# First attention layer of an audio tower: softmax sums inverted by VectorE block transposes, exponentials pre-added on GpSimd, weight scale from ScalarE sums

## The chip, the core and the metric

One NeuronCore of a Trainium2 chip runs the whole program. Its five engines have queues of their own: TensorE (PE, with its weight loads as PEld), VectorE (DVE), ScalarE (ACT), GpSimd (POOL) and SyncE (SP), which here only issues DMAs. Each engine executes its queue strictly in the order in which the program wrote it, and semaphores tie the queues together. The metric is the device time of one execution in microseconds; the median of three runs is 1176.59 us (1174.29 to 1178.07).

## The reference, cut to what matters

The input x has the shape (64, 96, 512): for each of 64 samples 32 channels of q, of k and of v over 512 positions. The first layer is an attention without heads over these, and it is the only part that the change touches:

```python
weight = jnp.einsum('bct,bcs->bts', q * scale, k * scale)   # 64 x 512 x 512
weight = jax.nn.softmax(weight, axis=-1)
h = jnp.einsum('bts,bcs->bct', weight, v)                   # 64 x 32 x 512
```

Then h, seen as 2048 rows of 512, goes through a layer norm, grouped-query attention with rotary embedding within each sample's 32 rows, a residual, a second layer norm and a gated feed-forward layer whose weights are quantized to -1, 0 and 1 by a threshold that is half the mean of |w|:

```python
h = h + attn(layernorm(h), Wq, Wk, Wv, Wo)
h = h + bitlinear(sigmoid(bitlinear(x, w1)) * bitlinear(x, w2), w3)
```

The preparation of both sets of weights runs inside the first part of the kernel.

## The kernel before, in words

The program has two stages. `token_attention` computes the first layer for 16 groups of four samples and prepares the weights beside it; `blocks` then runs the two other layers over 16 tiles of 128 rows. Between them all engines meet at a barrier. Only `token_attention` is changed.

**One group in `token_attention`.** A group has 16 score tiles of 128 x 512 in each of two forms. The *row* form (`rows`, line 469) has a query position on each partition and serves only to find the maximum of each row on VectorE (`maximum`, line 334). The *column* form (`cols`, line 492) has key positions on the partitions; two more rows of its operands carry the negated maxima, so ScalarE can take exponentials straight from PSUM (`exps`, line 293). q and k are split into a high and a low part so that 96 contraction rows of one fp32r product carry the precision: ScalarE rounds (`split_high`, line 287), GpSimd subtracts (`split_low`, line 248), and six SBUF to SBUF DMAs interleave the parts (`stack`, lines 175 to 180). The tiles `raw`, `high` and `low` are separate, so the next `load_qk` (line 166) waits only for `lo_done`.

**Values and sums.** For each of four blocks of key positions `values` (line 512) multiplies the exponentials by v, into OUT, and once more by a matrix of ones, into DEN: eight calls per group, at the steps of `VALUES_AT`. Each call is four fp32 matmuls of 32 output partitions. Then DEN has to be inverted and brought into the layout of OUT: ScalarE copies DEN and OUT to SBUF (lines 324 and 327), TensorE picks one row per sample and transposes it (`pick`, line 488, 16 matmuls with 4 columns), VectorE takes the reciprocal of 128 x 16 (`invert`, line 357), TensorE spreads it again (`spread_inverses`, line 521, 16 matmuls with 128 columns), and VectorE multiplies (`finish`, line 363).

**The order of work** is written out by hand. TensorE runs a loop of 16 steps per group (`step`, line 526). Step u of loop g issues one row tile and one column tile: at u = 2 to 11 rows 6 to 15 of group g+1, at u = 12 to 17 rows 0 to 5 of group g+2, and columns u of group g (u = 16 and 17 are columns 0 and 1 of group g+1). Row tiles go through a ring of three PSUM banks (`enter_ring`, line 463), so row tile n waits until VectorE has reduced row tile n-3. Column tiles have three banks too. The picks and spreads of group g-1 come at u = 4 and 5 of loop g. VectorE's loop (line 444) finishes rows 14 and 15 of group g+1, splits the maxima (lines 340 and 343), then reduces rows 0 to 13 of group g+2, with `take_transposed` (line 352) behind row 1, `invert` behind row 8 and `finish` behind row 9.

**Weights.** The attention weights (20 pieces of 128 x 1024) stay in SBUF; in loops 0 to 4 VectorE finds their largest magnitude (`largest`, line 367), and from loop 6 GpSimd scales them (`scale_attn`, line 253), ScalarE rounds them to fp16 (`attn_high`, line 305) and GpSimd computes the rest (`attn_low`, line 257). The feed-forward weights (12 pieces of 128 x 1408) are loaded twice: in loops 0 to 5 ScalarE sums their magnitudes (`measure_ffn`, line 298), and from loop 6 VectorE makes them ternary with two passes per piece (`below`, line 372, `above`, line 377). Before loop 6 VectorE runs `scales` (line 380), a chain of small operations with two GpSimd reductions over the partitions inside it.

## Time and profile before

| | |
|---|---|
| median of 3 runs | 1176.59 us (1174.29 to 1178.07) |
| profiled execution, its own time | 1181.81 us |
| its span, first to last instruction | 1179.9 us |
| PE busy in the span | 1097.3 us (93%) |
| DVE, POOL, ACT busy | 722.2, 433.5, 422.4 us |
| `token_attention` | 0 to 395.7 us, when the first load of `blocks` is issued |
| mean granted TensorE clock | 0.964 of full speed |

A busy share is an average over both stages. Matmuls are pipelined and their ends are modelled, so a busy PE need not be one that works at its peak. In a row of the trace the number in front is the start, the next one the duration; what stands in brackets is the idle time before it and what ended it. The granted clock is given as a share of full speed, 2.4 GHz; 0.5 is the lower level, 1.2 GHz.

### The profile page before, as it was taken

The numbers are of one execution on the slowest core, as the hardware profiler recorded it, in microseconds if no ns is written. First come the engines' busy times: TensorE is split into PE (matmuls) and PEld (weight loads), VectorE is DVE, ScalarE is ACT, GpSimd is POOL, SyncE is SP. The second block draws the span as 40 slices with busy tenths as digits, with TensorE's granted clock in tenths as the row PEclk, the third lists the DMA queues.
The fourth block names the chain that finished last, engine by engine and source line by source line (L and its number), as shares of the span: only waits on it lengthen the run. The fifth ranks groups of instructions, "written<-read, shape, count | busy, mean of one in ns | idle before, by whom it ended". The sixth has DMA issues, their size and how long they took to land.

```text
span 1179.9 us, 22172 instructions
## 1 busy us (share of the span) xinstructions
PE 1097.3 (93%) x8768; PEld 609.3 (52%) x8768; DVE 722.2 (61%) x1293; ACT 422.4 (36%) x733; POOL 433.5 (37%) x334
## 2 busy tenths in 40 slices
PE   4999998889989569999999999999999999999987
PEld 2434333343334234664665756646646657566465
DVE  6687766766686255556655755665566557656642
ACT  1666545545555221322322412323223223223231
POOL 2001016664555254242351451433423614524320
PEclk9999898989998779999999999999999999999999
DMA  6988833554442100000000000000000000000000
GB/s 181 315 298 260 299 115 115 158 176 124 140 130 69 57 9 10 20 9 27 18 9 27 0 27 18 9 27 18 9 27 18 9 27 0 27 18 9 18 11 9
DMA packets 35767, 83.81 MB, mean 71 GB/s; under 512 B 4496, under 2 KB 5264, under 8 KB 35728
## 3 DMA queue, kind: packets, MB, share of 16 engines
q1 hardware_dynamic: 35728, 83.26, 22.8%
q8 instruction: 27, 0.44, 0.2%
q14 instruction: 12, 0.10, 0.0%
HBM read 49.43 MB, written 8.39 MB: 49 GB/s over the span
## 4 chain that ended last, share of the span: by engine, by line
PE 51%; DVE 8%; issue 4%; POOL 2%; ACT 0%; DMA 0%; SPq 0%; DVEq 0%; POOLq 0%
PE proj L973 7%; PE proj L974 7%; PE proj L975 7%; PE ffn_sum L1025 5%; PE ffn_sum L1026 5%; PE proj L1087 4%; PE proj L1088 4%; PE proj L1089 4%; PE transposed L967 3%; PE ffn_sum L1073 2%; PE transposed L1041 1%; PE proj L1059 1%; PE proj L1060 1%; DVE probs_t L930 1%; DVE scores L910 1%
## 5 line engine op out<-in xcount | busy, mean ns | idle before, releaser
L334 DVE TENSOR_REDUCE row_max<-score_rows 128x1 f32<-128x512 f32 x256 | 167.7, 686 | 94.0 <-PE score_rows L474 92.6
L700 POOL TENSOR_TENSOR roped<-rope_cos,rope_sin 128x512 f32<-128x512 f32 x80 | 101.7, 1271 | 328.3 <-DVE rope_sin L836 328.3
L293 ACT ACTIVATE exps<-score_cols 128x512 f32<-128x512 f32 x256 | 146.2, 600 | 140.4 <-PE score_cols L499 137.9
L1025 PE MATMUL ffn_sum<-x_hi,ffn_w 128*128 128x128 f16 x1408 | 167.0, 220 | 1.4 <-ACT x_hi L769 1.4
L1026 PE MATMUL ffn_sum<-x_lo,ffn_w 128*128 128x128 f16 x1408 | 166.8, 220 | 0.0
L735 ACT ACTIVATE squares<-proj 128x512 f32<-128x512 f32 x80 | 47.8, 597 | 323.4 <-PE proj L975 289.5
L973 PE MATMUL proj<-attn_slots,x_hi 128*128 128x512 f16 x384 | 147.8, 385 | 3.7 <-DVE rope_sin L836 2.2
L974 PE MATMUL proj<-attn_slots,x_hi 128*128 128x512 f16 x384 | 147.7, 385 | 0.0
L975 PE MATMUL proj<-attn_slots,x_lo 128*128 128x512 f16 x384 | 147.5, 384 | 0.0
L474 PE MATMUL score_rows<-k_parts,q_parts 96*128 96x512 f32 x256 | 127.4, 511 | 16.5 <-DMA k_parts<-qk_low 15.2
L1025 PEld LDWEIGHTS ffn_sum<-x_hi,ffn_w 128*128 128x128 f16 x1408 | 138.1, 98 | 6.4 <-DVE hidden L853 3.0
L1026 PEld LDWEIGHTS ffn_sum<-x_lo,ffn_w 128*128 128x128 f16 x1408 | 138.5, 98 | 2.3
L474 PEld LDWEIGHTS score_rows<-k_parts,q_parts 96*128 96x128 f32 x256 | 53.7, 211 | 133.8 <-DVE row_max L334 72.6
L499 PE MATMUL score_cols<-q_parts,k_parts 98*128 98x512 f32 x256 | 110.2, 436 | 8.8 <-DMA q_parts<-max_t 6.9
L1087 PE MATMUL proj<-attn_slots,ctx_hi 128*128 128x512 f16 x256 | 97.0, 379 | 2.6 <-DVE ctx_lo L867 2.6
L1089 PE MATMUL proj<-attn_slots,ctx_lo 128*128 128x512 f16 x256 | 97.0, 379 | 0.0
L1088 PE MATMUL proj<-attn_slots,ctx_hi 128*128 128x512 f16 x256 | 97.0, 379 | 0.0
L248 POOL TENSOR_TENSOR qk_low<-qk_raw,qk_high 128x1024 fp32r<-128x1024 f32 x16 | 38.9, 2431 | 149.2 <-ACT qk_high L287 149.2
L707 POOL TENSOR_TENSOR roped<-roped,rms_inv 128x512 f32<-128x512 f32 x80 | 83.3, 1041 | 11.5
L703 POOL TENSOR_TENSOR rms_inv<-mean_sq,minus_half 128x4 f32<-128x4 f32 x80 | 85.2, 1065 | 3.3
L832 DVE TENSOR_TENSOR rope_cos<-proj,tables 128x512 f32<-128x512 f32 x80 | 55.1, 689 | 47.2 <-ACT squares L735 47.1
L853 DVE SCALAR_TENSOR_TENSOR hidden<-tanh,ffn_sum 128x512 f32<-128x512 f32 (+1 forms) x48 | 30.8, 641 | 85.7 <-PE ffn_sum L1026 85.7
(108 smaller groups left out, 1724.7 us busy)
## 6 DMA issues: line engine op xcount, KB each, us to landing
raw_ffn<-in_w_ffn SPq DMA_DIRECT2D x24, 704.0 KB, 7.2
attn_slots<-in_w_attn SPq DMA_DIRECT2D x20, 512.0 KB, 10.8
qk_raw<-in_qk SPq DMA_DIRECT2D x16, 512.0 KB, 5.8
q_parts<-qk_high SPq DMA_DIRECT2D x32, 256.0 KB, 3.3
k_parts<-qk_high SPq DMA_DIRECT2D x32, 256.0 KB, 4.2
v_t<-in_v_t SPq DMA_DIRECT2D x16, 256.0 KB, 5.7
q_parts<-qk_low SPq DMA_DIRECT2D x16, 256.0 KB, 4.9
k_parts<-qk_low SPq DMA_DIRECT2D x16, 256.0 KB, 5.2
```

What stands on the lines that cost most here:

```text
L293: nc.scalar.activation(E[:, (STEPS * g + u) % NE, :], ST[(STEPS * g + u) % 3][:, :], ACT.Exp, scale=TOK_SCALE).then_inc(exp_done, 1)
L334: nc.vector.reduce_max(row_max[:, g % 2, k:k + 1], S[n % NS][:, :], AX.X).then_inc(s_free, 1)
L474: nc.tensor.matmul(bank[:, :], QP[g % NB][0:3 * CH, b, t * P:(t + 1) * P], KP[g % NB][0:3 * CH, b, :], start=True, stop=True).then_inc(s_f ...
L499: nc.tensor.matmul(ST[n % 3][:, :], KP[g % NB][0:3 * CH + 2, b, i * P:(i + 1) * P], QP[g % NB][0:3 * CH + 2, b, :], start=True, stop=True) ...
L973: nc.tensor.matmul(dst, ah, bh, start=(i == 0), stop=False)
L974: nc.tensor.matmul(dst, ah, bl, start=False, stop=False)
L975: t = nc.tensor.matmul(dst, al, bh, start=False, stop=(i == len(pairs) - 1))
L1025: nc.tensor.matmul(dst, w, x2h[:, k * P:(k + 1) * P], start=(k == 0), stop=False)
L1026: ins = nc.tensor.matmul(dst, w, x2l[:, k * P:(k + 1) * P], start=False, stop=(k == KD - 1))
L1087: nc.tensor.matmul(PROJ[1][:, :], ah, bh, start=(k == 0), stop=False)
L1088: nc.tensor.matmul(PROJ[1][:, :], ah, bl, start=False, stop=False)
L1089: ins = nc.tensor.matmul(PROJ[1][:, :], al, bh, start=False, stop=(k == HEADS - 1))
```

## The change

It does seven things, all in `token_attention`.

1. **Inverse of the sums.** `pick`, `spread_inverses` and both ScalarE copies go. VectorE transposes DEN in 32 x 32 blocks into `den_t`, takes the reciprocal of one column of each block, transposes a broadcast of it back (`turn_sums`, `invert`), and multiplies OUT, now read in PSUM, by it (`finish`). These stand behind rows 8, 9 and 10.
2. **Pre-added exponentials.** GpSimd adds the exponentials of key blocks 0 and 1 (`sum_pair`), and in groups with `DEPTH` 2 (0 to 7, 14 and 15) those of block 2 (`sum_third`). TensorE multiplies the sum by the ones once (`total(g, None)`); the blocks left over go one by one. `values` becomes `weigh` (OUT, steps 8, 10, 13, 17) and `total` (DEN, steps 15 and 18 at depth 2, steps 12, 15 and 18 at depth 1; step 18 is step 2 of the next loop).
3. **Bound of the attention weights.** VectorE's `largest` goes; ScalarE sums the magnitudes (`bound_attn`), two or three pieces a loop in loops 0 to 7.
4. **Scaling of the attention weights.** GpSimd's `scale_attn` goes; ScalarE writes the scaled piece twice, once as fp16 and once as fp32, in loops 9 to 15.
5. **Ternary pass.** One piece per loop in loops 8 to 13, and three each in loops 14 and 15; the three of loop 15 stand behind the last `finish`. `scales` moves from loop 6 to loop 8.
6. **One in-place tile for the split.** `raw`, `high` and `low` become one tile `qk_split`; low overwrites raw. `load_qk(g)` now waits until the six copies of group g-1 have landed.
7. **SP's order.** Weight loads for loop g+1 are issued in loop g and ahead of `load_qk(g + 3)`; the last ternary loads stand ahead of the last `store_h`.

```diff
...
-        PICK_AT, SPREAD_AT = 4, 5
-        VALUES_AT = [7, 9, 10, 11, 13, 15, 16, 17]
-        SPLIT_AT = 14
         EARLY = 14
-        MEASURE_AT, CONVERT_AT = [12, 16], [11, 16]
-        MEASURED = 6
+        MEASURED = 8
         SCALED = 14
-        A_MEASURED = [range(4 * g, 4 * g + 4) if g < A_CHUNKS // 4 else () for g in range(NG)]
-        F_MEASURED = [range(2 * g, 2 * g + 2) if g < MEASURED else () for g in range(NG)]
-        A_CONVERTED = [range(2 * (g - MEASURED), 2 * (g - MEASURED) + 2) if g >= MEASURED else () for g in range(NG)]
-        F_CONVERTED = [()] * MEASURED + [(0,), (1,), (2,), (3,), (4,), (5,), (6, 7), (8, 9), (10,), (11,)]
+        SPLIT_AT = 13
+        A_MEASURE_AT, F_MEASURE_AT, CONVERT_AT = (3, 8, 12), (5, 15), (3, 12, 16)
+        A_MEASURED = shares([2, 3] * 4 + [0] * 8)
+        F_MEASURED = shares([2, 1] * 4 + [0] * 8)
+        A_CONVERTED = shares([0] * 9 + [2, 3, 3, 3, 3, 3, 3])
+        F_CONVERTED = shares([0] * 8 + [1] * 6 + [3, 3])
+        BEFORE_TAIL = 6
+        DEPTH = [2] * 8 + [1] * 6 + [2] * 2
+        SUMS_BEFORE = [sum(GB * d for d in DEPTH[:g]) for g in range(NG + 1)]
+        DENS_BEFORE = [sum(NT - d for d in DEPTH[:g]) for g in range(NG + 1)]
+        OUT_AT = {8: 0, 10: 1, 13: 2, 17: 3}
+        DEN_AT = {1: {12: None, 15: 2, 18: 3}, 2: {15: None, 18: 3}}
...
             def load_qk(g):
-                if g > 0:
-                    sp.wait_ge(lo_done, g)
-                sp.dma_start(raw[:, :, :], qk[g, :, :, :]).then_inc(qk_in, DMA)
+                if g == 2:
+                    sp.wait_ge(stacked[0], copies(0))
+                elif g > 2:
+                    sp.wait_ge(stacked[(g - 1) % 2], copies(g - 1))
+                sp.dma_start(split_raw(g), qk_raw[g, :, :, :]).then_inc(qk_in[g % 2], DMA)
...
             for g in range(NG):
                 if g + 2 < NG:
                     stack(g + 2)
+                if 0 < g and g + 1 < NG:
+                    load_v(g + 1)
+                for c in A_MEASURED[g + 1] if g + 1 < NG else ():
+                    load_attn(c)
+                for c in F_MEASURED[g + 1] if g + 1 < NG else ():
+                    measure_ffn(c)
+                early = F_CONVERTED[g] if g < NG - 2 else F_CONVERTED[g][:2] if g == NG - 2 else ()
+                for c in early:
+                    convert_ffn(c)
                 if g + 3 < NG:
                     load_qk(g + 3)
-                if 0 < g and g + 1 < NG:
-                    load_v(g + 1)
-                for c in F_MEASURED[g]:
-                    measure_ffn(c)
-                for c in F_CONVERTED[g]:
-                    convert_ffn(c)
-                for c in A_MEASURED[g]:
-                    load_attn(c)
                 if g > 0:
                     store_h(g - 1)
                 if g + 1 < NG:
                     store_max(g + 1)
+                for c in F_CONVERTED[g][len(early):]:
+                    convert_ffn(c)
             store_h(NG - 1)
             sp.wait_ge(h_out, NG * DMA)
...
+            def sum_pair(g, b):
+                pool.wait_ge(exp_done, STEPS * g + GB + b + 1)
+                if g > 0 and b == 0:
+                    pool.wait_ge(den_done, DENS_BEFORE[g - 1] + 1)
+                first = (STEPS * g + b) % NE
+                second = (STEPS * g + GB + b) % NE
+                nc.gpsimd.tensor_tensor(SUM[:, b, :], E[:, first, :], E[:, second, :], ALU.add).then_inc(summed, 1)
+
+            def sum_third(g, b):
+                pool.wait_ge(exp_done, STEPS * g + 2 * GB + b + 1)
+                pool.wait_ge(summed, SUMS_BEFORE[g] + b + 1)
+                third = (STEPS * g + 2 * GB + b) % NE
+                nc.gpsimd.tensor_tensor(SUM[:, b, :], SUM[:, b, :], E[:, third, :], ALU.add).then_inc(summed, 1)
...
+                for c in A_CONVERTED[g][:1]:
+                    attn_low(c)
+                for b in range(GB):
+                    sum_pair(g, b)
+                if DEPTH[g] == 2:
+                    for b in range(GB):
+                        sum_third(g, b)
                 if g == MEASURED:
                     reduce_partitions()
-                for c in A_CONVERTED[g]:
-                    scale_attn(c)
-                for c in A_CONVERTED[g][:1]:
+                for c in A_CONVERTED[g][1:2]:
                     attn_low(c)
                 if g + 3 < NG:
-                    split_low(g + 3)
-                for c in A_CONVERTED[g][1:]:
+                    lower(g + 3)
+                for c in A_CONVERTED[g][2:]:
                     attn_low(c)
...
+            def bound_attn(c):
+                act.wait_ge(a_in[c % NA], DMA * (c // NA + 1))
+                nc.scalar.activation(W.attn[:, 0:A_CHUNK], W.raw(c), ACT.Abs, accum_out=bound[:, c:c + 1]
+                                     ).then_inc(a_stat, 1)
...
             def attn_high(c):
-                act.wait_ge(a_scaled, c + 1)
+                act.wait_ge(chain, SCALED)
                 if c > 0:
                     act.wait_ge(a_lo, c)
-                nc.scalar.copy(W.hi(c * A_CHUNK, A_CHUNK), W.raw(c)).then_inc(a_hi, 1)
+                scale = scale_of[:, c:c + 1]
+                nc.scalar.activation(W.hi(c * A_CHUNK, A_CHUNK), W.raw(c), ACT.Copy, scale=scale).then_inc(a_hi, 1)
+                nc.scalar.activation(W.raw(c), W.raw(c), ACT.Copy, scale=scale).then_inc(a_scaled, 1)
...
+            def turn_sums(g):
+                dve.wait_ge(den_done, DENS_BEFORE[g + 1])
+                nc.vector.transpose(den_t[:, :, :].rearrange("p k c -> p (k c)"), DEN[:, :]).then_inc(den_turned, 1)
+
             def invert(g):
-                n = ring["pick", g]
-                dve.wait_ge(s_full, n + 1)
-                nc.vector.reciprocal(rden[:, :, :].rearrange("p i b -> p (i b)"), S[n % NS][:, 0:STEPS]
-                                     ).then_inc(s_free, 1)
+                dve.wait_ge(den_turned, g + 1)
+                nc.vector.reciprocal(rden[:, :], den_t[:, :, 0]).then_inc(inverted, 1)
+                dve.wait_ge(inverted, g + 1)
+                nc.vector.transpose(den_t[:, :, :].rearrange("p k c -> p (k c)"),
+                                    rden[:, :].unsqueeze(2).to_broadcast([P, STEPS, CH])).then_inc(inverse_out, 1)
 
             def finish(g):
-                dve.wait_ge(spread, g + 1)
-                dve.wait_ge(sums_out, 2 * g + 2)
-                nc.vector.tensor_tensor(out[:, :], out[:, :], DEN[:, :], ALU.mult).then_inc(h_done, 1)
...
+                dve.wait_ge(inverse_out, g + 1)
+                dve.wait_ge(out_done, NT * (g + 1))
+                if g > 0:
+                    dve.wait_ge(h_out, DMA * g)
+                nc.vector.tensor_tensor(out[:, :], OUT[:, :], den_t[:, :, :].rearrange("p k c -> p (k c)"), ALU.mult
+                                        ).then_inc(h_done, 1)
...
+                    for c in F_CONVERTED[g] if k == 3 and g < NG - 2 else ():
+                        below(c)
+                    for c in F_CONVERTED[g] if k == 5 and g < NG - 2 else ():
+                        above(c)
+                    for c in F_CONVERTED[g][:2] if k == 5 and g == NG - 2 else ():
+                        below(c)
+                        above(c)
+                    if k == 8:
+                        turn_sums(g)
+                    if k == 9:
                         invert(g)
-                    if k == PICK_ROW:
+                    if k == 10:
                         finish(g)
+                for c in F_CONVERTED[g][2:] if g == NG - 2 else F_CONVERTED[g] if g == NG - 1 else ():
+                    below(c)
+                    above(c)
...
+            def weigh(g, i):
+                if i == 0:
                     if g > 0:
-                        pe.wait_ge(sums_out, 2 * g)
+                        pe.wait_ge(h_done, g)
                     pe.wait_ge(v_in[g % NV], DMA * (g // NV + 1))
                 pe.wait_ge(exp_done, STEPS * g + GB * (i + 1))
                 for b in range(GB):
-                    into, by = (DEN, ones[:, :]) if sums else (OUT, VT[g % NV][:, i, b * CH:(b + 1) * CH])
-                    last = nc.tensor.matmul(into[b * CH:(b + 1) * CH, :], by, E[:, (STEPS * g + GB * i + b) % NE, :],
-                                            start=(i == 0), stop=(i == NT - 1))
...
+                last.then_inc(out_done, 1)
+
+            def total(g, i):
+                if i is None:
+                    if g > 0:
+                        pe.wait_ge(den_turned, g)
+                    pe.wait_ge(summed, SUMS_BEFORE[g + 1])
+                else:
+                    pe.wait_ge(exp_done, STEPS * g + GB * (i + 1))
+                for b in range(GB):
+                    of = SUM[:, b, :] if i is None else E[:, (STEPS * g + GB * i + b) % NE, :]
+                    last = nc.tensor.matmul(DEN[b * CH:(b + 1) * CH, :], ones[:, :], of, start=(i is None),
+                                            stop=(i == NT - 1))
+                last.then_inc(den_done, 1)
...
+                if u in OUT_AT:
+                    weigh(g, OUT_AT[u])
+                if u in DEN_AT[DEPTH[g]]:
+                    total(g, DEN_AT[DEPTH[g]][u])
+                if g > 0 and u + STEPS in DEN_AT[DEPTH[g - 1]]:
+                    total(g - 1, DEN_AT[DEPTH[g - 1]][u + STEPS])
...
```

## Rows read from the trace of the kernel before

**Rows 1.** The page's slices: granted clock, tenths of full speed, 40 slices.

```profile
PEclk9999898989998779999999999999999999999999
```

**Rows 2.** Busy time from finish to finish: PE, PEld, DVE, ACT, POOL; clock, DMA.

```profile
56.27:75.98 19.71, 19.71 (x140) 8.37 (x139) 16.12 (x27) 13.43 (x23) 2.39 (x1) 1.00 0.83 273
...
216.42:239.78 23.36, 21.28 (x139) 9.20 (x139) 16.27 (x23) 12.91 (x21) 13.55 (x6) 0.94 0.49 141
...
359.55:377.88 18.33, 18.33 (x129) 7.33 (x130) 12.05 (x16) 11.67 (x20) 6.18 (x3) 0.95 0.17 56
```

**Rows 3.** TensorE in time order, loop 1: start, duration, instruction.

```profile
50.36 0.40 PE L499 MATMUL score_cols<-q_parts,k_parts 98*128 98x512 f32 x1
...
51.69 0.50 PE L474 MATMUL score_rows<-k_parts,q_parts 96*128 96x512 f32 x1
52.03 0.40 PE L499 MATMUL score_cols<-q_parts,k_parts 98*128 98x512 f32 x1
52.26 0.40 PE L474 MATMUL score_rows<-k_parts,q_parts 96*128 96x512 f32 x1
...
55.68 0.50 PE L474 MATMUL score_rows<-k_parts,q_parts 96*128 96x512 f32 x1
```

**Rows 4.** Groups by line: count | busy us, mean ns | idle us.

```profile
L700 POOL TENSOR_TENSOR roped<-rope_cos,rope_sin 128x512 f32<-128x512 f32 x80 | 101.7, 1271 | 328.3 <-DVE rope_sin L836 328.3
...
L248 POOL TENSOR_TENSOR qk_low<-qk_raw,qk_high 128x1024 fp32r<-128x1024 f32 x16 | 38.9, 2431 | 149.2 <-ACT qk_high L287 149.2
...
L305 ACT CAST attn_slots<-attn_slots 128x1024 f16<-128x1024 f32 x20 | 20.8, 1038 | 8.0 <-POOL attn_slots L253 8.0
...
L372 DVE TENSOR_SCALAR ffn_w<-raw_ffn,w_nthr_of 128x1408 f16<-128x1408 f32 x12 | 14.3, 1190 | 0.0
...
L910 DVE STREAM_TRANSPOSE scores<-transposed 128x512 f32<-128x512 f32 x16 | 11.5, 717 | 12.6 <-PE transposed L1041 12.6
...
L357 DVE RECIPROCAL tok_rden<-score_rows 128x16 f32<-128x16 f32 x16 | 4.1, 258 | 13.7 <-PE score_rows L488 13.4
```

**Rows 5.** All engines in time order around one `above`.

```profile
208.59 2.14 POOL L257 TENSOR_TENSOR attn_slots<-attn_slots 128x1024 f16<-128x1024 f32 x1
...
208.69 3.53 DVE L377 SCALAR_TENSOR_TENSOR ffn_w<-raw_ffn,w_thr_of,ffn_w 128x1408 f16<-128x1408 f32 x1
...
212.14 1.87 DVE L334 TENSOR_REDUCE row_max<-score_rows 128x1 f32<-128x512 f32 x3
...
212.97 1.03 PE L488 MATMUL score_rows<-tok_ident,tok_den_sum 128*128 128x4 f32 x8 [2.08 <-DVE row_max L334]
```

**Rows 6.** Busy time and granted clock after that wait, same columns as group 2.

```profile
212.50:216.00 3.50, 3.03 (x42) 2.61 (x42) 2.47 (x5) 0.60 (x1) 3.50 (x2) 0.80 1.06 321
216.00:219.50 3.50, 3.50 (x21) 1.62 (x14) 2.08 (x3) 1.19 (x2) 1.75 (x1) 0.71 0.67 259
```

**Rows 7.** One line of VectorE, `above`: duration min/median/max.

```profile
L377 DVE SCALAR_TENSOR_TENSOR ffn_w<-raw_ffn,w_thr_of,ffn_w x12: 1675/3315/3527, 185.2 to 379.6; 128x1408 f16<-128x1408 f32 x12
```

**Rows 8.** VectorE in time order around `scales`.

```profile
166.42 0.34 DVE L384 TENSOR_REDUCE w_amax<-w_amax 128x1 f32<-128x8 f32 x4
...
171.41 1.29 DVE L334 TENSOR_REDUCE row_max<-score_rows 128x1 f32<-128x512 f32 x2
```

**Rows 9.** The page's DMA issues: count, KB each, median us to landing.

```profile
raw_ffn<-in_w_ffn SPq DMA_DIRECT2D x24, 704.0 KB, 7.2
attn_slots<-in_w_attn SPq DMA_DIRECT2D x20, 512.0 KB, 10.8
qk_raw<-in_qk SPq DMA_DIRECT2D x16, 512.0 KB, 5.8
...
k_parts<-qk_low SPq DMA_DIRECT2D x16, 256.0 KB, 5.2
```

**Rows 10.** All engines in time order at the end of the stage.

```profile
392.51 0.69 DVE L363 TENSOR_TENSOR tok_out_sum<-tok_out_sum,tok_den 128x512 f32<-128x512 f32 x1 [1.29 <-PE tok_den L521]
...
395.67 0.34 SPq L673 DMA_DIRECT2D h_ln<-h_rows  x1
```

More of the change, by code:

```diff
@@ L67, in ternary, with shares, token_attention @@
         return self.ffn[:, c * F_CHUNK:(c + 1) * F_CHUNK]
-LOOK, MAXIMA_AT, PICK_ROW = 6, 2, 9
+LOOK, MAXIMA_AT = 6, 2
 def score_ring():
     order = {}
-    for period in range(NG + 2):
+    for period in range(NG + 1):
         rows = [("row", period, k) for k in range(STEPS)] if period < NG else []
         maxima = [("max", period - 1)] if 1 <= period <= NG else []
-        pick = [("pick", period - 2)] if period >= 2 else []
-        for entry in rows[:MAXIMA_AT] + maxima + rows[MAXIMA_AT:PICK_ROW] + pick + rows[PICK_ROW:]:
+        for entry in rows[:MAXIMA_AT] + maxima + rows[MAXIMA_AT:]:
             order[entry] = len(order)
     return order
-def token_attention(nc, qk, vt, h1, ident_in, W, w_attn, w_ffn):
+def shares(counts):
+    ends = [sum(counts[:n + 1]) for n in range(len(counts))]
+    return [range(end - count, end) for count, end in zip(counts, ends)]
+def token_attention(nc, qk_raw, vt, h1, ident_in, W, w_attn, w_ffn):
     with ExitStack() as ctx:
@@ L100, in token_attention @@
         VT = [sb(f"v_t{n}", [P, NT, P]) for n in range(NV)]
[L101 to L102 removed]
+        qk = sb("qk_split", [P, 4, T])
         E = sb("exps", [P, NE, T])
+        SUM = sb("exp_sums", [P, GB, T])
         ident = sb("tok_ident", [P, P])
@@ L423, in scales @@
                 link(last)
-            def weights(g, k):
-                if k in (1, 5, 9, 13) and A_MEASURED[g]:
-                    largest(A_MEASURED[g][k // 4])
-                for n, c in enumerate(F_CONVERTED[g]):
-                    if k == (3, 10)[n]:
-                        below(c)
-                    if k == (5, 12)[n]:
-                        above(c)
             nc.vector.memset(ones[:, :], 1.0).then_inc(const_set, 1)
@@ L481, in transpose_maxima @@
                                  start=True, stop=True).then_inc(s_full, 1)
-            def pick(g):
-                pe.wait_ge(sums_out, 2 * g + 1)
-                bank = enter_ring(ring["pick", g])
-                first = ident[:, :].rearrange("p (b c) -> p b c", c=CH)[:, :, 0]
-                for i in range(NT):
-                    last = nc.tensor.matmul(bank[:, i * GB:(i + 1) * GB], den[:, i * P:(i + 1) * P], first,
-                                            start=True, stop=True)
-                last.then_inc(s_full, 1)
             def cols(g, u):
@@ L549, in _ @@
             cols(0, 1)
-            for g in range(NG + 1):
+            for g in range(NG):
                 for u in range(2, STEPS + 2):
-                    if g < NG:
-                        step(g, u)
-                    if u == PICK_AT and g > 0:
-                        pick(g - 1)
-                    if u == SPREAD_AT and g > 0:
-                        spread_inverses(g - 1)
+                    step(g, u)
+            total(NG - 1, NT - 1)
 TOK = 64 * 32
```

198 lines of the change are left out of this document (106 added, 92 removed).

## The prediction, made before the changed kernel was run

> **What bounds the kernel now.** I read the slices first, to see where the granted clock leaves its full level: only in the first third, which is `token_attention` [rows 1]. The second stage is not touched by the change, so all that counts is the first 395.7 us. Cut from one `finish` to the next, that stage gives 15 loops. A loop with nothing in its way takes 19.7 us, PE is busy in all of it, and VectorE, ScalarE and GpSimd are not (16.1, 13.4 and 2.4 us) [rows 2]. So TensorE's content is the bound there. The loops with ternary passes take about 23.4; of the six whole ones five lie between 23.2 and 23.4 [rows 2].
>
> Why 23.4 and not 19.7: VectorE's `above` stands 3.5 us instead of 1.7, because a GpSimd subtraction had begun 0.1 us before it; the row ring runs dry and PE idles 2.08 us [rows 5, 7]. Then the clock falls to its lower level: the two stretches behind it show 0.80 and 0.71, so 0.20 x 3.5 + 0.29 x 3.5 = 1.7 us of full-speed work is lost [rows 6]. 19.7 + 2.1 + 1.7 = 23.5. This is the pattern for what follows: a wait of 2 us of PE costs nearly 4.
>
> **What the change takes off TensorE.** From a column tile ahead of a `values` call to the row tile behind it are 1.33 us instead of 0.23, and the next pair costs 0.34 instead of 0.23: 1.2 us per call. From the row tile at 52.26 to that at 55.68 are 3.42 us; six row and column tiles of 0.235 are 1.41, so `pick` and `spread_inverses` are 2.0 [rows 3]. At depth 2 eight calls become six: 2.4 + 2.0 = 4.4 off, 15.3 us of PE content. At depth 1 seven are left: 16.5 us.
>
> **What takes its place.** The first `weigh` of a loop (u = 8) waits for `h_done` of the group before. VectorE reaches it through this chain: row tile 7 is issued behind the last `total`, 1.7 us into the loop, its maximum starts at 2.2; maxima 7 to 10 take 4 x 0.6 (three in 1.87, [rows 5]); two block transposes at 0.72 and a reciprocal at 0.26 [rows 4]; the multiply 0.69 [rows 10]; about 0.2 for semaphores, less about 0.3 that neighbours overlap. 2.2 + 2.4 + 1.4 + 0.3 + 0.7 = 7.0 us. PE gets there after 1.7 + 5.5 pairs of 0.47 = 4.3 to 4.5. So it idles 2.5 us, in order, with every row and column tile queued behind the waiting matmul, and ScalarE behind those. Before, `pick` and `finish` had no such chain and the loop had no wait. And 2.5 us is longer than the 2.08 after which the clock fell, so I add 1.7.
>
> **GpSimd's share.** It ran one instruction in a measuring loop; now there are eight additions of 1.27 us and the subtraction of 2.4 [rows 4], 12.6 us, two thirds of the loop. They hide beside PE: pairs end near 9 us, thirds near 13.5, `total` asks for them at u = 15, about 15 us in. What isn't hidden is the wait of VectorE for them. The row for `above` shows median 3.3 against a minimum of 1.7 [rows 7]. The second max split and `above` read two SBUF tiles; the split stands right ahead of the transposition of the maxima on PE. No row shows a split beside a GpSimd instruction: the ends are nothing (no loop is longer, as none was) and two instructions of 1.27, 2.5 us per loop. I take 0.6, half an addition, since GpSimd is idle a third of the time and PE has a little slack. By the Trainium skill (SBUF — State Buffer, Who interferes with whom) a VectorE instruction with two SBUF inputs and a GpSimd instruction that reads SBUF exclude each other for the whole of the one that came first, while a reduction never takes part; the 3.5 us row agrees, and by that rule the block transposes and `finish` stay free, but each split can lose up to a whole addition.
>
> Measuring loop: 15.3 + 2.5 + 1.7 + 0.6 = 20.1 us. Converting loop: 16.5 + 2.5 + 1.7 + 0.6, and for `below` and `above` beside a GpSimd with 3 x 2.1 + 4 x 1.27 + 2.4 = 13.9 us of work [rows 4, 5] another 0.8 (ends 0 and 4.5, one subtraction each; the low value, since PE's two calls at u = 17 and 18 leave VectorE 3 us to catch up): 22.1.
>
> **ScalarE** is busy 13.4 and 12.9 us in the two kinds of loop [rows 2]. It loses two copies of 0.6 and gains 2.5 sums while it measures (about 1.2 us each, an estimate from the pass of 1.04); while it converts it makes six passes of 1.04 us over a piece instead of two [rows 4]: about 15 and 16 us in 20 and 22, hidden, as column tiles have three banks of lead.
>
> **The in-place tile.** `load_qk` now waits for the copies: rounding 1.0, subtraction 2.4, two SP issues 1.3, landing 5.2, then the load 5.8 [rows 4, 9]: 15.7 us round, under 20. Weight loads issued ahead of it push it back; with their 10.8 [rows 9] in place of 5.8 it is 20.7, just at the loop. I take no cost.
>
> **Sum,** finish to finish. Start-up and loop 0: five calls for eight save 3.6, but loop 1 now meets the 2.5 us wait before its `finish` and the first loads stand in line: finish(0) at 56, as before (56.3). Seven measuring loops: 7 x 20.1 = 141, to 197 (before 216.4). Loop 8 with `scales`: 22.1 + 5.0 (166.42 to 171.41, [rows 8]) = 27, to 224. Five converting loops: 110, to 334 (before 359.6). Loops 14 and 15 took 33.0 (359.55 to 392.51, [rows 2, 10]); their PE content falls by 2 x 4.4, but two ternary pieces ahead of `turn_sums(14)` take 5.8 and ScalarE (14 x 0.55 + 6.2 us) sets loop 15: 30, to 364 (before 392.5).
>
> **The tail.** Three ternary pieces now stand behind the last `finish`, and the third's load waits for the first: 2.9 (1.2 + 1.7, [rows 4, 7]) + load + 2.9. The load's median is 7.2 under traffic [rows 9]; on an empty queue I take 5 (ends nothing, were it there already, and 7.2). The last `store_h` stands behind it on SP and is hidden. Stage end 10.8 after `finish` ends, before 2.5 (393.2 to 395.67, [rows 10]): +8.3.
>
> 364.0 + 0.7 + 10.8 = 375.5 against 395.7: 20 us less. The profiled execution took 1181.8, so 1162 like for like; it lies 5.2 above the median of the runs, and the forecast for the median is 1176.6 - 20 = 1157 us.
>
> **Rivals.**
> - *The clock stays up* (0.22). For: one undisturbed kind of loop kept 1.00, and a wait of 2 us need not always be followed by a fall. Against: the converting loops, all at 0.92 to 0.94 (one of them in [rows 2]). 13 loops x 1.7 = 22 less: 1135. With the transposes quicker than costed, down to 1125.
> - *GpSimd holds VectorE up everywhere* (0.14), the slower side. Place: the splits ahead of the maxima's transposition in every loop, and `below` and `above` in six. Price: 2.4 instead of 0.6 in 14 loops is 25, 3.5 instead of 0.8 in six is 16; partly the same wait, so 30 of 41: 1187. It decides against the change once it takes more than 20 us, an average of 1.4 us per loop above my 0.6. By the skill's rule named above this is what happens whenever the order is unlucky; by the rows it happened to at least half of the `above` (median 3.3).
> - *The round of the in-place tile is the loop* (0.17). If weights push the load to landings of 12 to 13 us, the round is 22.5: 2.4 more in seven loops, 17: 1174, near no change. Against: less weight data per loop (2.5 and 1.5 pieces instead of 4 and 2).
> - Something else, both ways, 0.05; the forecast itself 0.42.
>
> **Range and chances.** A measurement here can tell about 0.3%, 3.5 us, from no change. Faster: 0.40 of the forecast's 0.42, all of the first rival, 0.11 of the third, 0.03 of the rest: 0.76. Slower: 0.13 of the second, 0.02 and 0.01 of third and rest, 0.16 in all; same 0.08. The range runs from the first rival's lower part to where the second's begins: 1128 to 1183.
>
> **What would show it.** Right: PE waits of 2 to 3 us ahead of the first `weigh` of each loop, put down to VectorE's `finish`; the granted clock at 0.9 to 0.95 in the measuring loops too; measuring loops near 20 and converting loops near 22 us; some 10 us between the last `finish` and the first load of the second stage. Wrong: measuring loops of 18 us or less at full clock; splits of 1 us and more; ScalarE's rounding waiting for `qk_raw` in most loops; a second stage of another length than 784 us.

## The result, and the profile after

The change makes the kernel slower: 1191.7 us median (4 runs, 1188.1 to 1198.5) against 1177.3 (4 runs beside them), ratio 1.0124, 95% interval 1.0085 to 1.0163. The forecast was 1157. The profiled execution of the changed kernel took 1192.1 us, span 1190.2.

| stretch of stage 1, us | before | predicted | after | split freed (a1) | best (d4) |
|---|---|---|---|---|---|
| start to `finish(0)` | 56.3 | 56 | 62.9 | 56.8 | 57.2 |
| seven measuring loops | 160.1 | 141 | 147.6 | 129.0 | 130.7 |
| loop 8, with the scales | 23.4 | 27 | 29.5 | 28.7 | 28.6 |
| five converting loops | 119.8 | 110 | 108.6 | 109.5 | 108.5 |
| loops 14 and 15 | 33.0 | 30 | 46.7 | 44.7 | 36.7 |
| last `finish` to the first load of stage 2 | 3.2 | 11.5 | 10.9 | 10.9 | 3.2 |
| stage 1 ends | 395.7 | 375.5 | 406.1 | 379.7 | 364.8 |

The inner rows are each a difference of two `finish` starts in one profiled execution; what follows stage 1 takes 782.6 to 785.9 us in every profiled execution. In the kernel before, `scales` stands in loop 6 and converting starts there, so its "seven measuring loops" hold that loop (30.4 us) and a converting one (23.4), and its loop 8 has no scales. Three stretches came out far above the forecast: the start (by 6.9 us), the seven measuring loops (6.6), and loops 14 and 15 (16.7). The five converting loops were as said.

Busy time from `finish` to `finish` of the changed kernel, with the columns of [rows 2]: PE, PEld, DVE, ACT, POOL; clock, DMA:

```profile
62.85:83.81 20.96, 17.16 (x82) 7.13 (x82) 14.57 (x24) 13.97 (x26) 12.29 (x10) 0.92 0.74 236
126.25:145.68 19.43, 15.63 (x82) 6.60 (x82) 14.46 (x24) 14.06 (x26) 12.31 (x10) 1.00 0.77 248
239.93:260.54 20.61, 17.88 (x93) 6.78 (x91) 17.11 (x26) 14.33 (x23) 12.29 (x8) 1.00 0.55 159
348.50:373.70 25.20, 18.40 (x70) 5.81 (x70) 17.03 (x18) 12.49 (x20) 15.61 (x11) 0.67 0.13 42
373.70:395.22 21.52, 12.93 (x58) 3.46 (x57) 4.92 (x7) 12.53 (x18) 16.67 (x12) 0.76 0.24 80
```

TensorE's content is down as costed (15.6 us where [rows 2] show 19.7), but in these rows no engine is busy all through a loop any more: each waits for another at some point. The slices of the profile show it as clock; in [rows 1] the first third read higher:

```profile
PEclk9889988798877588999999999999999999999999
```

What is waited for shows in the lines of the two operations of the split (duration min/median/max; below, who waited for them, us and times). `max_parts` took 175 ns before:

```profile
L423 DVE TENSOR_SCALAR max_parts<-row_max x16: 174/684/5762, 24.4 to 356.7; 128x16 fp32r<-128x16 f32 x16
...
L426 DVE SCALAR_TENSOR_TENSOR max_parts<-row_max,max_parts x16: 174/175/1289, 24.6 to 362.5; 128x16 fp32r<-128x16 f32 x16
  PEld score_rows L569: 27.5, 11
  PE score_rows L569: 22.4, 10
```

And in time order, from loops 0, 1 and 14 of the changed kernel, these instructions alone (start, duration, instruction, idle time before it):

```profile
42.55 4.92 POOL L316 TENSOR_TENSOR exp_sums<-exp_sums,exps 128x512 f32<-128x512 f32 x4
43.04 4.47 DVE L423 TENSOR_SCALAR max_parts<-row_max 128x16 fp32r<-128x16 f32 x1
47.54 0.17 DVE L426 SCALAR_TENSOR_TENSOR max_parts<-row_max,max_parts 128x16 fp32r<-128x16 f32 x1
47.77 0.63 PE L569 MATMUL score_rows<-tok_ident,max_parts 128*32 128x128 f32 x2 [4.56 <-DVE max_parts L426]
...
66.36 4.96 POOL L316 TENSOR_TENSOR exp_sums<-exp_sums,exps 128x512 f32<-128x512 f32 x4
67.99 0.92 DVE L423 TENSOR_SCALAR max_parts<-row_max 128x16 fp32r<-128x16 f32 x1
68.94 1.19 DVE L426 SCALAR_TENSOR_TENSOR max_parts<-row_max,max_parts 128x16 fp32r<-128x16 f32 x1
...
355.44 4.95 POOL L316 TENSOR_TENSOR exp_sums<-exp_sums,exps 128x512 f32<-128x512 f32 x4
356.73 5.76 DVE L423 TENSOR_SCALAR max_parts<-row_max 128x16 fp32r<-128x16 f32 x1
360.35 2.12 POOL L321 TENSOR_TENSOR attn_slots<-attn_slots 128x1024 f16<-128x1024 f32 x1
362.76 0.64 PE L569 MATMUL score_rows<-tok_ident,max_parts 128*32 128x128 f32 x2 [6.32 <-DVE max_parts L426]
```

A VectorE operation that runs on while GpSimd works is called held here. Every hold ends within 40 ns of the end of a GpSimd instruction: 0.92 and 1.19 us to the end of one addition, but 4.47 and 5.76 us to the end of the whole run, that is, of the GpSimd instructions that stand back to back. TensorE waits behind it, in order (4.56 and 6.32 us). Of the sixteen first operations nine were held, five of them past at least one end of an addition, to the end of the run; of the second ones three, each to the next end.

### The profile page after: what moved, and what is told of

It is laid out like the page before. It is cut to its first block, busy times and chain, and to the rows that moved or that the text cites. A ratio compares the mean times of both kernels' runs of the same rounds, so it can differ in the third digit from the quotient of the medians.

```text
span 1190.2 us, 20779 instructions
## 1 busy us (share of the span) xinstructions
PE 1055.7 (89%) x7920; PEld 582.0 (49%) x7920; DVE 727.0 (61%) x1305; ACT 444.4 (37%) x761; POOL 495.3 (42%) x418
## 4 chain that ended last, share of the span: by engine, by line
PE 51%; DVE 8%; issue 4%; POOL 2%; ACT 0%; DMA 0%; SPq 0%; DVEq 0%; POOLq 0%
PE proj L1053 7%; PE proj L1054 7%; PE proj L1055 7%; PE ffn_sum L1105 5%; PE ffn_sum L1106 5%; PE proj L1167 4%; PE proj L1168 4%; PE proj L1169 4%; PE transposed L1047 3%; PE ffn_sum L1153 2%; PE transposed L1121 1%; PE proj L1139 1%; PE proj L1140 1%; DVE probs_t L1010 1%; DVE scores L990 1%
## 5 line engine op out<-in xcount | busy, mean ns | idle before, releaser
L374 ACT ACTIVATE exps<-score_cols 128x512 f32<-128x512 f32 x256 | 141.5, 598 | 137.1 <-PE score_cols L579 135.8
L579 PE MATMUL score_cols<-q_parts,k_parts 98*128 98x512 f32 x256 | 116.4, 461 | 21.6 <-ACT exps L374 17.0
L310 POOL TENSOR_TENSOR exp_sums<-exps 128x512 f32<-128x512 f32 x64 | 79.7, 1277 | 67.7 <-ACT exps L374 67.7
L589 PE MATMUL tok_out<-exps,v_t 128*32 128x512 f32 x512 | 84.9, 741 | 12.0 <-DVE tok_out_sum L453 11.8
L787 POOL TENSOR_TENSOR roped<-roped,rms_inv 128x512 f32<-128x512 f32 x80 | 83.2, 1040 | 11.5
```

Of the source, the lines that this page charges most:

```text
L374: nc.scalar.activation(E[:, n % NE, :], ST[n % 3][:, :], ACT.Exp, scale=TOK_SCALE).then_inc(exp_done, 1)
L579: nc.tensor.matmul(ST[n % 3][:, :], KP[g % NB][0:3 * CH + 2, b, i * P:(i + 1) * P], QP[g % NB][0:3 * CH + 2, b, :], start=True, stop=True) ...
```

## The experiments

The theory after this reading (theory 1): the splits, held beside the additions, are the loss. Rivals: the additions' own latency on the path, the tail, the start, the inverse. Medians and ratios are against the kernel before on the same chip.

**a1, the two split operations written as reductions** (for this the row maxima and their two parts share one tile; nothing else changed):

```diff
-nc.vector.tensor_scalar(max_parts[:, 0, :], row_max[:, g % 2, :], -1.0, None, ALU.mult)
+nc.vector.tensor_reduce(m[:, 1, :].bitcast(F32R), m[:, 0, :].unsqueeze(2), AX.X, ALU.max, negate=True)
-nc.vector.scalar_tensor_tensor(max_parts[:, 1, :], row_max[:, g % 2, :], -1.0, max_parts[:, 0, :], ...)
+nc.vector.tensor_reduce(m[:, 2, :], m[:, 0:2, :].rearrange("p j k -> p k j"), AX.X, ALU.add, negate=True)
```

> The changed kernel, but the two small operations that split the row maxima are written as reductions with a negated output, same engine, same place, same results. In the changed kernel they stand 20.3 and 5.9 us in sum instead of 2.8 each, the longest 5.8 us beside four GpSimd additions in a row. Theory 1 (GpSimd's additions hold VectorE, and TensorE behind the maxima): a reduction isn't held, both operations fall to 0.2 us each, and of the 20 us gained 12 to 30 leave the time (with the clock that falls behind each wait), most of it in loops 0 and 14: about 1174 us. Theory 2 (the loop is set by the wait for `finish` ahead of the first `weigh`, and VectorE's other waits lie beside it): what is gained ahead of the maxima is lost again there, less than 5 us in all: 1187 us or more.

Measured: 1166.5 us (4 runs), ratio 0.9918 [0.9888, 0.9948]: 25 us less than the changed kernel. Its first split, and two of its measuring loops:

```profile
L423 DVE TENSOR_REDUCE max_parts<-max_parts x16: 170/170/171, 24.3 to 331.2; 128x16 fp32r<-128x16 f32 x16
```

```profile
76.01:93.88 17.87, 15.72 (x82) 6.62 (x82) 12.71 (x24) 14.07 (x26) 12.34 (x10) 1.00 0.83 258
111.76:130.94 19.18, 17.11 (x82) 7.13 (x82) 12.80 (x24) 14.27 (x26) 12.28 (x10) 0.91 0.85 275
```

GpSimd does the same 12.3 us per loop, VectorE the same list; only the kind of the two 16-column operations differs. The splits had run 20.6 us above 32 x 0.175: 4.3 of them ahead of `finish(0)`, 9.5 in the seven measuring loops, 5.6 in loop 14. What came back is 6.0, 18.6 and, in loops 14 and 15, 2.0 us. So the measuring loops gave back about twice the length of their holds; the granted clock was 0.78 to 1.00 in them with the holds and 0.91 to 1.00 without. This does not go loop by loop: loop 6 (166.56 to 187.16) has no held split and was 2.8 us longer than in a1, behind a stretch at a granted clock of 0.52 to 0.57 (166.5 to 174). Theory 1 holds, but the gain does not lie where it was expected, in loops 0 and 14: most of it lies between them.

**a4, the changed kernel without GpSimd's additions** (all sums on TensorE, 31 us more content):

> The changed kernel without GpSimd's additions: TensorE multiplies each of the four blocks of exponentials by the ones, at steps 9, 12, 15 and 18. TensorE gets 10 x 2.4 + 6 x 1.2 = 31 us more content. Theory 1: VectorE's held time goes at once (about 20 us ahead of the maxima and 5 at the ternary passes, with the clock), so the sum is 1190 to 1200. Theory 2 (what GpSimd holds is hidden): all 31 us show, 1215 to 1225.

Measured: 1175.5 us (10 runs), ratio 0.9993 [0.9975, 1.0012]. Both theories had it at 1190 or more; it is some 15 us faster than that. None of its 32 split operations was held (0.18 us at most), which bears theory 1 out. The additions as they were built cost 16 us; with the split freed they earn 9 (a1 against a4). They earn it in the measuring loops (129.0 us for 142.3) and give part of it back where the expectation had no cost: loop 8 takes 23.7 us in a4 and 28.7 in a1, loops 14 and 15 take 39.1 and 44.7. In loop 8 the two reductions of `scales` stand behind the additions in GpSimd's program; in the changed kernel VectorE waited 4.6 us for them, in a4 1.1.

**a2, the three last ternary pieces ahead of the last transpose of the sums**, and **c1, a1 with a2 and the first feed-forward weights loaded behind the first store of the maxima:**

> The changed kernel, but the three ternary pieces of loop 15 are converted ahead of the last block transpose instead of behind the last `finish`. VectorE idles 16.5 us there. Theory (the tail is on the path): the 10.2 us from the last `finish` to the first load of the second stage become 2.5 to 3, so 7 to 8 us off: about 1184 us. Rival: the last piece's load comes too late and holds the last transpose instead, so that under 2 us are gained.

> The first two edits together, and a third: the feed-forward weights of loop 0 are loaded behind the first `store_max` instead of ahead of it, since the first column tile waits 4.1 us for that store. If the three costs lie in different places they add up: 18 + 8 + 3 = 29 us, about 1163 us, which would beat the kernel before (1177). Theory 2 gives 1187 - 8 - 3 = 1176.

Measured: a2 1190.3 us, ratio 1.0109 [1.0082, 1.0137]; c1 1165.5, 0.9899 [0.9874, 0.9924]. Neither is distinguishable from its base (the changed kernel, and a1), where 7 to 8 us were expected of the tail. In c1 `finish(0)` starts at 57.3, as in a1 (56.8): the late first store costs nothing that I can show. The tail falls to 3.2 us in both, and loop 15 takes most of it back: 27.3 us for 21.5 in a2, 27.5 for 21.0 in c1. (The profiled execution of c1 took 1174.3 us, 9 above its median, so its measuring loops are not compared.) From the trace of a2, with other instructions left out:

```profile
386.64 2.57 DVE L464 SCALAR_TENSOR_TENSOR ffn_w<-qk_split,w_thr_of,ffn_w 128x1408 f16<-128x1408 f32 x1
387.69 8.33 POOL L316 TENSOR_TENSOR exp_sums<-exp_sums,exps 128x512 f32<-128x512 f32 x4
391.12 2.56 DVE L464 SCALAR_TENSOR_TENSOR ffn_w<-raw_ffn,w_thr_of,ffn_w 128x1408 f16<-128x1408 f32 x1
396.17 1.94 PE L605 MATMUL tok_den<-exp_sums,tok_ones 128*32 128x512 f32 x8 [10.88 <-POOL exp_sums L316]
```

Four additions take 8.33 us for 4.9, VectorE's `above` 2.57 for 1.68: beside each other both lose, and TensorE waits 10.9 us for the sums. Instruction by instruction they take turns: the four additions took 2.64, 1.91, 2.64 and 1.26 us, and each of the first three waited for one VectorE pass that had been let in just before it. In the changed kernel itself the additions of these loops were not stretched (4.95 us per four); there the held split of 5.76 us stood in loop 14, and a shorter wait for the sums in loop 15:

```profile
388.95 1.93 PE L602 MATMUL tok_den<-exp_sums,tok_ones 128*32 128x512 f32 x8 [3.43 <-POOL exp_sums L316]
```

In a1, with the split free, the stretched additions take the place of the hold, and the wait is 4.85 and 5.15 us:

```profile
331.06 7.83 POOL L315 TENSOR_TENSOR exp_sums<-exp_sums,exps 128x512 f32<-128x512 f32 x4
339.04 1.93 PE L601 MATMUL tok_den<-exp_sums,tok_ones 128*32 128x512 f32 x8 [4.85 <-POOL exp_sums L315]
```

That is why a1 won only 2.0 us there. So, with the split free, the additions are what the last two loops wait for:

**d1, a1 with one level of additions in loops 14 and 15** (`DEPTH = [2] * 8 + [1] * 8`), and **d2, a1 with none there (`[2] * 8 + [1] * 6 + [0] * 2`) and the ternary pieces of a2:**

> The changed kernel with the split as reductions (1166.5 us), and in its last two loops one level of additions instead of two, as in loops 8 to 13. There the trace shows TensorE waiting 4.85 and 5.15 us for the second level of additions in loops 14 and 15, beside ternary pieces that take 3.6 us in place of 1.7. If these waits are what makes the two loops 44.7 us where 33.0 were before: they fall to about 40 us, and the kernel to 1161 to 1164 us. Rival (loops 14 and 15 are bound by the ternary pieces and the weight parts, whatever the depth): 1166 us.

> The changed kernel with the split as reductions, no additions in the last two loops, and the three last ternary pieces ahead of the last transpose of the sums instead of behind it. Theory: with the pieces inside alone, the additions of loop 15 ran 16 us for eight beside them and the last `finish` came 7 us later, so nothing was won; without additions there the pieces fill VectorE's idle time: loops 14 and 15 take 36 to 39 us, the tail 2.5 to 4 us in place of 10.9, and the kernel 1152 to 1157 us, faster than both. Rival (the pieces wait for their loads and for the slot, and hold the last `finish` up again): 1163 to 1168 us.

Measured: d1 1156.9 us, ratio 0.9866 [0.9822, 0.9910]; d2 1149.7, 0.9786 [0.9755, 0.9818]. Both are faster than expected. Loops 14 and 15 take 35.7 and 37.1 us (44.7 in a1), the tail 10.7 and 3.2. One level of additions fits into those loops with the last three pieces behind them, and those pieces fit once no additions are left there; two levels fitted in neither case.

**d3, d2 with one level of additions everywhere, and d4, d2 with the first `weigh` at step 9:**

> The fastest so far (split as reductions, ternary pieces inside, no additions in the last two loops: 1149.7 us) with one level of additions in loops 0 to 7 too, in place of two: eight groups of four sums more on TensorE, 8 x 1.06 us at the high clock, and 32 GpSimd additions fewer. If TensorE's content sets those loops: 3 to 8 us slower, 1153 to 1158 us. If GpSimd's hold on the remaining VectorE operations (`finish`, the copy of the maxima) sets them: 1144 to 1149 us.

> The fastest so far (1149.7 us) with the first product of a loop at step 9 in place of 8. In it TensorE and its weight loads still sat 27.1 us in all behind `finish` ahead of the first products (some 13 us on the matmul engine). Theory: one step later, about 1.2 us, covers that wait in most loops: 5 to 12 us less, 1138 to 1145 us. Rival (the wait only moves to the next product or to the exponentials, which need the slot that the product frees): 1147 to 1152 us.

Measured: d3 1158.8, 0.9851 [0.9813, 0.9890]: the second level is worth some 8 us by the two ratios, 6.7 of them in the measuring loops of the traces. d4 1148.8, 0.9764 [0.9726, 0.9803]: the same as d2, and not the 1138 to 1145 of its theory. What sat idle ahead of `weigh` in d2, then in d4 (us over PE and PEld, times):

```profile
  DVE tok_out_sum L452: 27.1, 22
```

```profile
  DVE tok_out_sum L452: 2.3, 5
```

The wait is gone and the time isn't: with a free split the time did not hang on it. Of d4, a measuring loop and the last one, which was 21.5 us:

```profile
57.17:75.05 17.88, 16.15 (x82) 6.62 (x82) 12.71 (x24) 13.74 (x26) 12.35 (x10) 1.00 0.87 277
343.06:361.61 18.55, 13.05 (x74) 3.47 (x73) 14.69 (x12) 12.53 (x18) 5.74 (x4) 0.82 0.40 132
```

d2 and d4 are faster than both kernels.

**b2, the kernel before with the block-transposed inverse alone; b7, that with its products at steps 9 to 13 and 15 to 17:**

```diff
-                nc.scalar.copy(den[:, :], DEN[:, :]).then_inc(sums_out, 1)
-                nc.scalar.copy(out[:, :], OUT[:, :]).then_inc(sums_out, 1)
...
+                    if k == PICK_ROW - 2:
+                        turn_sums(g)
```

> The kernel before with the change's inverse alone: no picks and spreads on TensorE, no copies of the sums on ScalarE, two block transposes and a reciprocal on VectorE. From the rows of before, a converting loop of 23.7 us holds 0.95 us of picks and 1.08 us of spreads at the high clock and twice that at the low one, and their waits. If loops follow TensorE's content: 1.5 to 3 us per loop, 25 to 45 us less, 1135 to 1150 us. Rival (the clock and the wait for `finish` ahead of the first weigh give it back, as the changed kernel's loops of 21 us where content alone gave 17 suggest): 8 to 15 us less, 1161 to 1168 us. Rival 2 (the wait of weigh for `finish` costs more than the pick): no faster than 1176 us.

> The kernel before with the block-transposed inverse alone (1193.5 us), and the eight groups of products with the exponentials at steps 9, 10, 11, 12, 13, 15, 16, 17 in place of 7, 9, 10, 11, 13, 15, 16, 17. With the inverse alone TensorE waited 2.46 us in every loop for `finish` ahead of the first product, and its clock fell behind that. Theory: the first product two steps later finds `finish` done, the wait and the low stretch go, the measuring loops fall from 23.8 to 19.7 to 21 us and the converting ones to 21.7 to 22.4 us: 1150 to 1163 us. Rival (the clock falls in every loop of less content whatever the wait, since ScalarE and VectorE then set the pace): 1180 to 1194 us.

Measured: b2 1193.5, ratio 1.0161 [1.0124, 1.0198]; b7 1196.2, 1.0168 [1.0128, 1.0208]. Both are over 30 us slower than their theories had them; b2's second rival and b7's rival come nearest. There are 42 matmuls fewer per loop, and in b2 most loops take 23.8 us, measuring and converting alike. The converting ones took about that before, so the loss lies in the measuring stretch, 173.3 us for 160.1. b2's wait ahead of the first product, and the same place in b7, with b7's busy time in the stretch around it:

```profile
81.75 1.94 PE L504 MATMUL tok_out<-exps,v_t 128*32 128x512 f32 x8 [2.46 <-DVE tok_out_sum L363]
```

```profile
82.55 0.80 PE L477 MATMUL score_rows<-k_parts,q_parts 96*128 96x512 f32 x1 [1.58 <-DVE row_max L328]
```

```profile
99.10:108.21 9.11, 6.33 (x28) 3.01 (x24) 9.08 (x15) 4.50 (x9) 0.00 (x0) 0.85 1.06 299
```

VectorE is busy 9.08 of 9.11 us there: transposes, multiply, row maxima and the 1.2 us maxima of the attention weights stand in one stretch. Moving the product only moves the wait onto the row ring. My theory for b7 fell: in this stretch VectorE sets the pace. Alone the inverse is a loss. The change also takes the weights' maxima off VectorE (12.7 us busy in a loop of a1, 17.3 in one of b7); that this is what makes the inverse pay there, or that it pays at all, is my reading and not shown, since no run has a1 or d2 without the inverse.

**b3 to b6, b8, b9: idle additions in the kernel before.** Forty GpSimd additions (eight in each of loops 0 to 4) on tiles that nothing reads:

```diff
+                pool.wait_ge(exp_done, STEPS * g + 8)
...
+                nc.gpsimd.tensor_tensor(spare[n % 4], spare[n % 4], spare[n % 4], ALU.add)
```

b4 releases the n-th of a loop by exponential 2n+1; b5 adds a1's split; b6 reads two different sources (1.27 us each, 1.04 with one); b8 and b9 shorten the first addition of a loop, which moves the point at which the split arrives.

> The kernel before with 40 idle GpSimd additions of 128x512 (in place, on tiles that nothing reads): eight in each of loops 0 to 4, all released by the eighth exponential of the loop, so that they run back to back over the split of the maxima. Nothing waits for them. Theory 1 (a held VectorE operation with two SBUF operands or in its two-port form waits for the whole run of GpSimd instructions): the first split operation, 175 ns in the kernel before, takes 4 to 8 us in each of these five loops, VectorE's slack there takes 1 to 2 us of it, and the kernel is 12 to 25 us slower than before: 1188 to 1201 us. Rival A (held for the one instruction that runs, 1.27 us at most): the split takes at most 1.3 us, the kernel 1176 to 1180 us. Rival B (the additions cost the path only through the sums that TensorE waits for, as in the changed kernel): nothing waits here, so 1176 us and the split at 175 ns.

> The same 40 idle additions, but the n-th of a loop released by exponential 2n+1, so that each of 1.27 us stands alone, some 1 us of idle GpSimd behind it. Theory 1: a held VectorE operation waits for the rest of one addition, 1.3 us at most; the split takes 0.2 to 1.3 us, 1176 to 1182 us. Rival (what counts is how many additions there are, or the memory traffic that they make): as slow as with the eight in a row.

> The eight idle additions in a row, and the two split operations written as reductions over the maxima tile. Theory 1: a reduction does not wait for GpSimd, the split stays at 0.17 to 0.2 us, and the kernel is within 4 us of before (1174 to 1180 us): `finish`, with one operand in SBUF and one in PSUM, and the copy of the transposed maxima are then all that might be held. Rival (the additions slow TensorE's or ScalarE's reads of SBUF): as slow as with the split as it was.

> The kernel before with the same eight idle additions in a row, but each with two different source tiles, as the changed kernel's additions have (1.24 us there; the in-place ones with one source took 1.04 us and held a split operation only to the end of the addition that ran: 0.83 and 0.96 us at most). Theory (additions with two different sources can keep a held VectorE operation out past the end of one of them, as in the changed kernel, where seven of the sixteen first split operations were held, five of them past at least one boundary, 4.47 and 5.76 us at most): additions of 1.24 us, the first split above 1.3 us in some of the loops 0 to 4, 1180 to 1190 us. Rival (the hold past a boundary comes from something else of the changed kernel): splits of at most 1.3 us each, 1176 to 1180 us.

> The kernel before with the eight idle additions in a row, the first of them shortened to 32, 96, 160, 224 and 288 columns in loops 0 to 4, so that the split of the maxima arrives at other points of a running addition: by the 1.25 us of a full one, some 0.2, 0.0, 1.1, 0.95 and 0.8 us after its start, where it was 0.3 us in all loops before. In the changed kernel a split that arrived 0.39 or 0.40 us after the start of an addition was let in at the next boundary, and those at 0.05, 0.49, 0.68, 0.72 and 0.74 us only at the end of the whole run. Theory (the point of arrival decides): the late arrivals of this kernel are held to the end of the run, 2 to 5 us. Rival (something else of the changed kernel decides): every split is let in at the next boundary, 1.25 us at most.

> The same with the first addition at 352, 384, 416, 448 and 480 columns: arrivals some 0.7, 0.6, 0.5, 0.45 and 0.4 us after the start of a running addition. Theory (the point of arrival decides): the first three or four of them are held to the end of the run, 2 to 5 us, the last at 0.4 us is let in at the next boundary. Rival: 1.25 us at most in each.

Three corrections to these: nine first splits, not seven, were held in the changed kernel; b3's theory of a wait for the whole run fell; and the theory of b8 and b9, that the point of arrival decides, did not fit a trace that was there already. In a2 splits that arrived 0.36 to 0.39 us after the start of an addition were held past two ends, to the end of the run (3.35 to 3.39 us, three times), and those at 0.69 and 0.70 were let in at the next end, the other way round than in the changed kernel. Measured: 1177.7, 1178.4, 1178.3, 1179.7, 1179.0 and 1178.0 us, ratios 1.0011, 1.0003, 1.0020, 1.0016, 1.0021 and 0.9983, none off by more than 0.3%. From the trace of b6, these instructions alone:

```profile
40.80 2.50 POOL L276 TENSOR_TENSOR attn_slots<-attn_slots,ffn_w 128x512 f32<-128x512 f32 x2
41.11 1.00 DVE L355 TENSOR_SCALAR max_parts<-row_max 128x16 fp32r<-128x16 f32 x1
42.14 1.20 DVE L358 SCALAR_TENSOR_TENSOR max_parts<-row_max,max_parts 128x16 fp32r<-128x16 f32 x1
43.27 2.51 POOL L276 TENSOR_TENSOR ffn_w<-ffn_w,attn_slots 128x512 f32<-128x512 f32 x2
```

In b3, b6, b8 and b9 39 of the 40 splits in those loops were held, each to the next end of an addition, 1.26 us at most, from whatever point; in b4 and b5 none was. Each pair lost up to 2 us, and the kernel before hardly notices: of the six intervals only b8's (1.0008 to 1.0035) lies off 1. So a hold is real and cheap here and dear in the changed kernel. I put that down to less TensorE content to hide it under and to holds past several ends; no run tells the two apart. Why some holds last to the end of the run is open: neither the number of additions in a row, nor the number of sources, nor the point of arrival explains it.

## Why the prediction was wrong, step by step

Stage 1 ended at 406.1 us for my 375.5, 30.6 late (rounded): the start 6.9, the measuring loops 6.6, loop 8 2.5, loops 14 and 15 16.7, less 2.0 in the converting loops and the tail.

- *TensorE's content.* Right: 15.6 us at full clock for my 15.3.
- *The split, "I take 0.6, half an addition", ends 0 and 2.5.* This step failed. In the seven measuring loops the term was 2.7 us a loop by a1 (18.6 in all), not 0.6. I looked for a hold of the second operation only, and 17.5 of the 20.6 us stand in the first, which has one input. Nine of the sixteen first ones were held, the longest 4.47 and 5.76 us, above my upper end, since I bounded one operation by one instruction and GpSimd runs four and more in a row. Freeing them gave back 25 us of kernel time. I had the mechanism as the rival with chance 0.14. Its 25 us for the splits are what a1 gave back; its total of 1187, near the measured 1191.7, is in part luck: it also put 16 us on `below` and `above`, where the converting loops were as forecast, and nothing on loops 14 and 15.
- By the Trainium skill (SBUF — State Buffer, Who interferes with whom) a VectorE operation with two SBUF inputs, beside a GpSimd instruction that reads SBUF, or one in a two-port mode, and GpSimd's instruction shut each other out, and a reduction takes no part. a1 agrees (5.76 us to 0.17), and so do the 39 holds. That section gives the one that issues first the shared ports "for the whole instruction"; by that each hold beside an addition would have been 1.3 us at most (an estimate, from additions of 1.27). The changed kernel measured 5.76, and the measurement decides.
- *The wait for `finish`, 2.5 us and 1.7 of clock per loop.* Too dear. b2 shows it as forecast (2.46 us), but in the changed kernel and in a1 it was 1.2 (in a1 27.2 us over 22 waits of PE and PEld, in eleven loops), and with the split free four of seven measuring loops kept the full clock: 18.4 us a loop for my 20.1. d4 shows that what is left of it costs nothing. This error, 12 us, hid part of the others: the measuring loops came out at 21.1, one us from my 20.1, as the sum of two errors.
- *Loops 14 and 15, "30".* Failed: 46.7. I costed TensorE and ScalarE there and not GpSimd. In the changed kernel the held split (TensorE waits 6.32 us) and the sums (3.43 us) are the waits on GpSimd's additions. With the split free the additions stretch beside the two-pass ternary pieces, four of them to 7.8 us in a1 (8.3 in a2), with TensorE's sums behind them; d1 took 9 of the 15 us that a1 was above my 30 back.
- *The tail, +8.3.* Right: 10.9 us against 3.2, +7.7.
- *The start.* 56.8 in a1: right but for the first held split.
- *Loop 8, 27.* Too cheap: 29.5, and 28.7 with the split freed. I had no cost for the additions that stand ahead of the reductions of `scales` in GpSimd's program; without them (a4) it took 23.7.
- *The in-place tile.* Right: measuring loops went down to 17.9 us in a1 with it in place.

With a1's split stage 1 ends at 379.7 for my 375.5. That is near by luck: the measuring loops are 12 us under my sum there, and loops 14 and 15 14.7 above it.

## What to carry to other kernels

Work given to GpSimd is priced by what VectorE has beside it, not by GpSimd's idle time: ask for each two-input or plain arithmetic VectorE operation on the path who waits for it, and bound its hold by the longest run of GpSimd instructions, not by one. A tiny operation can sometimes be written as a reduction, as here; so written, the split was never held. And an edit that moves work (here the inverse, from TensorE to VectorE) must be costed on the engine that receives it, in the stretch where it lands: alone it made this kernel 1.6% slower.

## What was not expected of the hardware

- A 16-column `tensor_scalar` with one input is held as well as an operation with two: 0.17 us became 5.76.
- A hold of the first split operation can outlast several GpSimd instructions (five of nine in the changed kernel, three of ten in a2), yet in 39 provoked cases no hold did.
- GpSimd loses as much as VectorE: an addition of 1.24 us took 2.08 beside `above` (8.33 us for four, 4.95 without), and `above` 2.57 for 1.68.
- A GpSimd addition of a tile to itself took 1.04 us, of two tiles 1.27.
